# The second router's rows prepared in the last attention round, its logits by column tiles and a selection product

## The chip, the cores and the metric

The kernel runs on one core of a Trainium2 chip. The metric is device microseconds of one execution: 1426.83 us is the median of 3 runs of the kernel before (1425.14, 1426.83 and 1431.81).

## What is computed

A two-layer decoder over 2048 rows of 256 values (`x`) with 1601 context rows of 512. Each layer adds a cross-attention part and a mixture of eight experts; the change lies between the second layer's attention and its experts. Cut to that, the reference is:

```python
# attention of the second layer: 8 heads of 32, queries are the normed rows
x = x + jnp.tanh(g_xattn[1]) * attention(ctx_2048, _layernorm(x), mask)
...
def _L1_ffn_ref(x, rw1, rb1, rw2, rb2, w1, b1, w2, b2):      # x is layernorm(x)
    logits = jax.nn.silu(jnp.einsum('bsd,dh->bsh', x, rw1) + rb1)      # 256 -> 1024
    logits = jnp.einsum('bsh,he->bse', logits, rw2) + rb2              # 1024 -> 8
    k_logits, k_index = jax.lax.top_k(logits, 2)
    k_prob = jax.nn.softmax(k_logits, axis=-1)
    ...
    for e in range(E):
        we = jnp.sum(jnp.where(k_index_f == e, k_prob_f, 0.0), axis=-1)
        h = jax.nn.silu(xf @ w1[e] + b1[e]) @ w2[e] + b2[e]
        out = out + we[:, None] * h
x = x + jnp.tanh(g_ffn[1]) * _L1_ffn_ref(_layernorm(x), ...)
```

## The kernel before, in words

The program is written engine by engine; each engine (TensorE or PE, VectorE or DVE, ScalarE or ACT, GpSimd or POOL, and SyncE or SP, which issues most transfers) has its own list in a fixed order, and semaphores tie them together. All data is f32. The 2048 rows are 16 chunks of 128, kept in X; four chunks are a query group.

Stages in order: loads and the first attention part (a recurrence over the context, to about 106 us of the span), the first router and its table, 23 slots of the first expert stage (to about 417), the second attention, the second router, 39 slots of the second expert stage.

**The second attention** runs in 8 rounds (`interleaved`): round n takes a query group n // 2 and four of the eight heads. A round has 13 steps, one for each block kc of 128 keys. In a step PE makes four score products (`scores`, 128x512 each, ScalarE turns them into exponentials in a ring PT of 16 tiles, half of it in Z1 and half in WS0) and the values' products of the step before (`values`: four products of 32 columns at the positions 0, 32, 64, 96 of the array, written to four quarters of PSUM tile PB6), and every second step the column sums of the exponentials (`summed`, the same form with ones). For the other steps POOL adds exponentials up (ACC in WS0 and WS1) and one sum of those ends the round. Between the scores stands the search for maxima of the next round (`maxima`, PE and DVE); the last round has no next one, so its steps hold scores, values and sums alone. Behind a round ScalarE copies the result out (`attended`), PE turns it (`turned_out`), and DVE divides it and adds it into X (`into_x`, eight parts in the steps 2 and 3 of the next round, with the row statistics of the group's four chunks in every second round).

**The second router** starts when the last round and its `into_x` are through. DVE and POOL make 1/std of all 16 chunks (`inv_std`, `power`). Then for each of four groups: for each of four chunks DVE norms the rows (XR, line 908), PE turns them (`turned`, line 277), DVE copies them to XG (line 913), one chunk after the other; SP also stores each XR to xn1, from which the experts gather. PE then makes eight hidden products (line 547: 2 matmuls of 128x512, RW1 against XG), ScalarE applies SiLU (line 1060, two tiles HR), and after each PE makes a logits product (`lm`, line 526: the 8 columns of rw2s against HR, 8 partitions of PB6, accumulated over eight). DVE copies the 8x512 result (LT, line 918) and four transposes (line 555) put the logits of 128 rows on 128 partitions of PB7. After four groups the routing (`route`, from line 686) and PE's table products (line 357) give the experts' slots.

`turned` takes its PSUM tile from a ring of three and waits until the reader of its last content is done. The order of PE's router is that of its loops; SP's order is the list of its transfers, and a wait in it holds what stands behind.

**The second expert stage** fetches about 2.2 MB of weights and bias a slot. The first slot's weights are fetched when the attention ends; those of the second wait for the table, as the gathers of rows do. Results are added into `out` by scattered transfers.

## Time and profile before

| what | us or share |
|---|---|
| median of 3 runs | 1426.83 |
| the profiled execution, its own time | 1423.83 |
| its span, first to last instruction | 1422.0 |
| PE busy, matmuls / weight loads | 1213.8 / 861.3 |
| DVE, ACT, POOL busy | 519.3, 465.7, 479.2 |
| mean granted clock of PE | 0.926 of full speed |

The page gives busy times of the engines over the whole span; the windows give the same by stage, with the granted clock and the transfers' share. The chain of waits is followed back from the last instruction, each step to what released it. A timeline row gives start, duration, engine, line, operation, tile written and tiles read, the number of instructions in the row, and in brackets the idle time before it with what ended it. A f32 matmul is two records there (a transposing one is one), with the numbers of operand rows and columns. PEld is the weight load of PE.

### The profile page before, as it was taken

The numbers are of one execution on the slowest core, as the hardware profiler recorded it, in microseconds if no ns is written. First come the engines' busy times: TensorE is split into PE (matmuls) and PEld (weight loads), VectorE is DVE, ScalarE is ACT, GpSimd is POOL, SyncE is SP. The second block draws the span as 40 slices with busy tenths as digits, with TensorE's granted clock in tenths as the row PEclk, the third lists the DMA queues.
The fourth block names the chain that finished last, engine by engine and source line by source line (L and its number), as shares of the span: only waits on it lengthen the run. The fifth ranks groups of instructions, "written<-read, shape, count | busy, mean of one in ns | idle before, by whom it ended". The sixth has DMA issues, their size and how long they took to land.

```text
span 1422.0 us, 19271 instructions
## 1 busy us (share of the span) xinstructions
PE 1213.8 (85%) x7094; PEld 861.3 (61%) x7094; DVE 519.3 (37%) x1255; ACT 465.7 (33%) x1067; POOL 479.2 (34%) x495
## 2 busy tenths in 40 slices
PE   2365899999977899999999999968875999999985
PEld 2245899999964444454544544322225888888885
DVE  1574222221127876675675765011114010101000
ACT  2011122221101355655655556611110333323331
POOL 0150111111103366576666755700001223223231
PEclk9885799999996699999999999989885999999998
DMA  6114587888841000000000000020001899999994
GB/s 195 48 60 148 205 295 285 295 295 323 306 170 40 1 1 1 1 16 0 1 16 1 1 16 1 0 93 15 26 4 61 290 337 304 315 306 302 331 304 132
DMA packets 53978, 197.08 MB, mean 139 GB/s; under 512 B 8539, under 2 KB 34397, under 8 KB 38013
## 3 DMA queue, kind: packets, MB, share of 16 engines
q1 hardware_dynamic: 39584, 173.25, 34.4%
q0 software_dynamic: 10464, 18.36, 5.4%
q10 hardware_dynamic: 3836, 4.24, 0.9%
q8 instruction: 57, 0.93, 0.3%
q14 instruction: 37, 0.30, 0.1%
HBM read 179.44 MB, written 16.38 MB: 138 GB/s over the span
## 4 chain that ended last, share of the span: by engine, by line
PE 59%; DMA 20%; DVE 10%; issue 5%; ACT 3%; POOL 1%; SPq 1%; ACTq 0%; POOLq 0%; DVEq 0%
DMA out<-Z,SI 18%; PE PQ L392 13%; PE PB L497 7%; PE PQ L482 6%; PE PB L406 6%; PE PB L466 5%; PE PQ L547 5%; PE PB L277 4%; PE PB L487 4%; DVE Z L852 3%; PE PQ L466 2%; PE PB L526 2%; PE PB L357 1%; DVE SM L568 1%; POOL SM L1084 1%
## 5 line engine op out<-in xcount | busy, mean ns | idle before, releaser
L392 PE MATMUL PQ<-Z,WS 128*128 128x128 f32 x2720 | 328.5, 277 | 11.9 <-issue 10.7
L392 PEld LDWEIGHTS PQ<-Z,WS 128*128 128x128 f32 x2720 | 323.0, 193 | 25.0 <-issue 18.9
L406 PE MATMUL PB<-WS,Z 128*128 128x256 f32 x992 | 234.3, 379 | 0.0
L852 DVE TENSOR_REDUCE Z<-PB 128x1 f32<-128x402 f32 x340 | 183.4, 567 | 87.1 <-PE PB L466 85.9
L406 PEld LDWEIGHTS PB<-WS,Z 128*128 128x128 f32 x992 | 179.1, 190 | 19.3
L482 PE MATMUL PQ<-QS,KS 128*128 128x512 f32 x416 | 173.0, 437 | 7.3 <-ACT Z L1041 4.5
L979 ACT ACTIVATE Z<-PQ,WS 128x128 f32<-128x128 f32 x312 | 89.2, 368 | 204.4 <-PE PQ L392 204.4
L466 PE MATMUL PB<-KS,QS 128*128 128x402 f32 x340 | 132.9, 403 | 15.7 <-DVE Z L852 6.8
L482 PEld LDWEIGHTS PQ<-QS,KS 128*128 128x128 f32 x416 | 77.1, 190 | 104.8 <-issue 56.6
L1041 ACT ACTIVATE Z<-PQ 128x512 f32<-128x512 f32 x208 | 109.6, 603 | 85.1 <-PE PQ L482 84.9
L1041 ACT ACTIVATE WS<-PQ 128x512 f32<-128x512 f32 x208 | 109.2, 604 | 79.4 <-PE PQ L482 79.4
L1103 POOL DMA_INDIRECT Z<-xn,SI x62 | 60.9, 983 | 218.0 <-DVE SM L749 199.8
L1110 POOL DMA_INDIRECT out<-Z,SI x39 | 61.9, 1588 | 207.5 <-DMA out<-Z,SI 177.9
L792 DVE TENSOR_TENSOR Z<-PB,Z 128x256 f32<-128x256 f32 x39 | 16.6, 424 | 284.9 <-PE PB L406 284.9
L1173 POOL TENSOR_TENSOR WS<-WS,Z 128x512 f32<-128x512 f32 x80 | 100.5, 1286 | 41.4 <-ACT Z L1041 41.4
L1173 POOL TENSOR_TENSOR WS<-WS 128x512 f32<-128x512 f32 x80 | 100.5, 1287 | 39.5 <-ACT WS L1041 39.5
L852 DVE TENSOR_REDUCE Z<-PQ 128x1 f32<-128x402 f32 x172 | 97.5, 567 | 43.8 <-PE PQ L466 43.2
L781 DVE TENSOR_TENSOR Z<-Z,PQ 128x512 f32<-128x512 f32 x46 | 31.6, 687 | 179.0 <-PE PQ L392 179.0
L466 PEld LDWEIGHTS PB<-KS,QS 128*128 128x128 f32 x340 | 67.7, 199 | 47.2 <-DVE Z L852 33.4
L1110 POOL DMA_INDIRECT yd<-Z,SI x23 | 22.7, 987 | 216.0 <-DVE Z L789 216.0
L975 ACT ACTIVATE Z<-PQ 128x512 f32<-128x512 f32 x46 | 27.5, 597 | 151.7 <-PE PQ L392 151.7
L466 PE MATMUL PQ<-KS,QS 128*128 128x402 f32 x172 | 69.6, 404 | 7.6 <-DVE Z L852 4.0
(238 smaller groups left out, 1246.2 us busy)
## 6 DMA issues: line engine op xcount, KB each, us to landing
WS<-in_w SPq DMA_DIRECT2D x62, 1024.0 KB, 6.8
WS<-in_w SPq DMA_DIRECT2D x23, 2048.0 KB, 8.1
WS<-in_w SPq DMA_DIRECT2D x39, 1028.0 KB, 7.5
Z<-in_b SPq DMA_DIRECT2D x39, 128.0 KB, 6.7
X<-in_x SPq DMA_DIRECT2D x4, 512.0 KB, 10.5
xn<-WS SPq DMA_DIRECT2D x16, 128.0 KB, 1.7
WS<-yd SPq DMA_DIRECT2D x4, 512.0 KB, 5.9
out<-X SPq DMA_DIRECT2D x4, 512.0 KB, 2.9
```

Of the source, the lines that this page charges most:

```text
L392: t = e.matmul(bank[:, j * P:j * P + P], w[:, k, o:o + P], FXT[i % 2][:, k * P:k * P + P], start=k == 0, stop=k == 1)
L406: t = e.matmul(y, FS[c % 4][:, j * P:j * P + P], w[:, 4 * n + j, :], start=n == 0 and j == 0, stop=n == 1 and j == 3)
L466: e.matmul(PB[b][:, 0:PIECE], q[:, h, t4 * P:t4 * P + P], KS[:, 4 * hf + h, s * PIECE:(s + 1) * PIECE], start=True, stop=True).then_inc(t_ ...
L482: e.matmul(PB[g % 3], KS[:, 4 * (n % 2) + hh, kc * P:kc * P + P], QS[n % 2][:, hh, :], start=True, stop=True).then_inc(t_s, 1)
L497: e.matmul(PB[6][32 * hh:32 * hh + 32, :], V[:, kc, (4 * hf + hh) * 32:(4 * hf + hh) * 32 + 32], PT[(g + hh) % 16], start=kc == 0, stop=kc ...
L547: t = e.matmul(PB[m % 3], RW1[:, k, f * P:f * P + P], XG[g % 2][:, k, :], start=k == 0, stop=k == 1)
L852: e.tensor_reduce(MP[j % 2][:, i:i + 1], PB[bank_of["pc", r]][:, 0:PIECE], AX.X, ALU.max).then_inc(v_pc, 1)
L979: t = e.activation(FS[c % 4][:, j * P:j * P + P], PB[c % 4][:, j * P:j * P + P], ACT.Silu, bias=WS[i % 2][:, o:o + 1])
L1041: e.activation(PT[g % 16], PB[g % 3], ACT.Exp).then_inc(a_p, 1)
L1103: e.indirect_dma_start(FXL[i % 4], None, xn, bass.IndirectOffsetOnAxis(ap=tabi[:, i:i + 1].bitcast(U32), axis=0)).then_inc(d_xl[l][i % 4], 16)
L1110: e.indirect_dma_start(into, bass.IndirectOffsetOnAxis(ap=tabi[:, i:i + 1].bitcast(U32), axis=0), FY[i % 2], None, **add).then_inc(d_y[l][ ...
L1173: e.tensor_tensor(acc, acc, PT[g % 16], ALU.add).then_inc(p_acc, 1)
```

## The change

What it does:

- XR, XG and HR move: XR and XG lie in WS1, XG has four tiles in place of two (one for each group), HR has eight tiles in Z1 in place of two.
- In the last round, steps 1 to 12, `prepared` turns the chunks 0 to 11 behind each step's scores. DVE norms chunk c+1, then copies chunk c out. The 1/std of these chunks is made ahead of them, that of chunks 12 to 15 after the round; POOL's power is split in two.
- PE's router becomes one stream over 32 hidden products (`hidden`). The turning of the last attention output stands behind the second one. The chunks 12 to 15 are turned behind the 13th to 16th.
- The logits are made in eight groups of four products in column tiles (`partial_logits`): product j of a group writes partitions 32j to 32j+31, and the second half of a query group accumulates on the first. The weights RW2 are rw2 padded from 8 to 32 columns.
- DVE copies all 128 partitions (LT, `partial`), and `logits_of` makes for each chunk one product of LT with a constant 128x8 selection (C_SEL), which adds the four parts up and turns them at once, in place of the transpose.
- rw2 is no longer loaded at the start (1024 pieces of 32 B); RW2 is fetched to V when the last values are read. SP stores chunks 0 to 11 during the last round, 12 to 15 and the last part of X behind the first slot's weights.
- `route` waits for the stores of xn1 ahead of its first write to WS1.

PE, the start of the last round (line numbers differ by 2; lines 484 and 482 are scores, 499 and 497 values, 513 and 511 with the following row the turning of the output before). Before:

```order
L482 MATMUL PQ<-QS,KS 128x512 x4
L497 MATMUL PB<-WS,V 32x512 x4
L511 MATMUL PB<-CT,Z 128x128 x4
L277 MATMUL PB<-CT,Z 128x128 x4
L482 MATMUL PQ<-QS,KS 128x512 x4
L497 MATMUL PB<-Z,V 32x512 x4
```

Now:

```order
L484 MATMUL PQ<-QS,KS 128x512 x4
L279 MATMUL PB<-CT,WS 128x128 x2
L499 MATMUL PB<-WS,V 32x512 x4
L513 MATMUL PB<-CT,Z 128x128 x4
L279 MATMUL PB<-CT,Z 128x128 x4
L484 MATMUL PQ<-QS,KS 128x512 x4
L279 MATMUL PQ<-CT,WS 128x128 x2
L499 MATMUL PB<-Z,V 32x512 x4
```

Two transposes of a prepared chunk (from WS) have come in behind the scores of each of twelve steps.

PE, from the last column sums (487, now 489) into the router (547 and 526, now 538 hidden and 550 logits, 560 selection). Before:

```order
L487 MATMUL PB<-WS,CT 32x512 x8
L511 MATMUL PB<-CT,Z 128x128 x4
L277 MATMUL PB<-CT,Z 128x128 x4
L277 MATMUL PQ<-CT,Z 128x128 x2
L277 MATMUL PB<-CT,Z 128x128 x4
L277 MATMUL PQ<-CT,Z 128x128 x2
L547 MATMUL PQ<-Z 128x512 x4
L526 MATMUL PB<-Z,SM 8x512
L547 MATMUL PQ<-Z 128x512 x2
L526 MATMUL PB<-Z,SM 8x512
```

Now:

```order
L489 MATMUL PB<-WS,CT 32x512 x8
L538 MATMUL PQ<-WS,Z 128x512 x4
L513 MATMUL PB<-CT,Z 128x128 x4
L279 MATMUL PB<-CT,Z 128x128 x4
L538 MATMUL PQ<-WS,Z 128x512 x8
L550 MATMUL PB<-Z,V 32x512 x4
L538 MATMUL PQ<-WS,Z 128x512 x8
L550 MATMUL PB<-Z,V 32x512 x4
L538 MATMUL PQ<-WS,Z 128x512 x4
L560 MATMUL PB<-CT,Z 128x8 x4
```

The hidden products follow the sums at once, with the turning of the output behind the second, and the logits come in fours.

SP, around the end of the attention (out<-X are stored parts of X, xn<- the stored normed rows, in_w and in_b the weights and bias of a slot, in_rw the router's weights). Before:

```order
L1268 DMA out<-X 128x4x256 x4
L1221 DMA WS<-in_w 128x2056
L1226 DMA WS<-in_w 128x2048
L1230 DMA Z<-in_b 128x256
L1275 DMA xn<-Z 128x256 x16
```

Now:

```order
L1310 DMA out<-X 128x4x256 x3
L1316 DMA xn<-WS 128x256 x12
L1322 DMA V<-in_rw 128x8x32
L1263 DMA WS<-in_w 128x2056
L1268 DMA WS<-in_w 128x2048
L1272 DMA Z<-in_b 128x256
L1316 DMA xn<-WS 128x256 x4
L1310 DMA out<-X 128x4x256
```

Twelve stores of rows went ahead of the first slot's weights, RW2 came in, and one store of X went behind them.

The diff, its core:

```diff
@@ -57,6 +58,7 @@
...
+    c[:, C_SEL:C_SEL + E] = j[:, None] % 32 == np.arange(E)[None, :]
...
@@ -160,10 +162,11 @@
...
-        XR = [Z1[:, 256 * i:256 * i + 256] for i in range(4)]
-        XG = [Z1[:, 1024 + 1024 * i:2048 + 1024 * i].rearrange("p (k q) -> p k q", k=2) for i in range(2)]
-        HR = [Z1[:, 3072 + 512 * i:3584 + 512 * i] for i in range(2)]
-        LT = Z0[0:8, 2048:2560]
+        XR = [WS[1][:, 5120 + 256 * i:5376 + 256 * i] for i in range(4)]
+        XG = [WS[1][:, o:o + 1024].rearrange("p (k q) -> p k q", k=2) for o in (2048, 3072, 4096, 0)]
+        HR = [Z1[:, 512 * i:512 * i + 512] for i in range(8)]
+        RW2 = VW[:, 2560:2816].rearrange("p (f e) -> p f e", e=32)
+        LT = Z0[:, 2048:2560]
...
@@ -249,16 +252,15 @@
...
+                    if n == 7 and kc:
+                        prepared(kc - 1)
...
-                if kc == 1 and n:
+                if kc == 1 and n and n < 8:
...
-            turned_out(7)
-            for part in range(8):
-                into_x(7, part)
...
@@ -515,46 +517,61 @@
             for _ in maxima(0):
                 pass
...
+            def prepared(c):
+                e.wait_ge(v_xr, c + 1)
+                turned(ring, ("xr", c), [XR[c % 4][:, k * P:k * P + P] for k in range(2)],
+                       (v_xg, c + 1)).then_inc(t_xr, 1)
+            interleaved(maxima, scores, values, lambda n: None, turned_out, lambda n, part: None, prepared)
+            def hidden(m):
+                g, f = divmod(m, 8)
+                if f == 0:
+                    e.wait_ge(v_xg, 4 * g + 4)
+                if m == 0:
+                    e.wait_ge(d_rw1, 16)
+                    e.wait_ge(a_p, 416)
+                if m >= 3:
+                    e.wait_ge(a_hr, m - 2)
+                for k in range(2):
+                    t = e.matmul(PB[m % 3], RW1[:, k, f * P:f * P + P], XG[g][:, k, :], start=k == 0, stop=k == 1)
+                t.then_inc(t_hr, 1)
+            def partial_logits(h):
+                g, half = divmod(h, 2)
+                e.wait_ge(a_hr, 4 * h + 4)
+                if h == 0:
+                    e.wait_ge(d_rw2, 16)
+                    e.wait_ge(a_ot, 8)
+                if half == 0 and g:
                     e.wait_ge(v_lt, g)
...
+                for j in range(4):
+                    t = e.matmul(PB[6][32 * j:32 * j + 32, :], RW2[:, 4 * half + j, :], HR[(4 * h + j) % 8],
+                                 start=half == 0, stop=half == 1, tile_position=(0, 32 * j))
+                t.then_inc(t_lm, 1)
+            def logits_of(g):
+                e.wait_ge(v_lt, g + 1)
+                if g == 0:
+                    e.wait_ge(v_rt, 8)
                 for t4 in range(4):
                     c = 4 * g + t4
...
+                    t = e.matmul(PB[7][:, c * E:c * E + E], LT[:, t4 * P:t4 * P + P], CT[:, C_SEL:C_SEL + E], start=True,
+                                 stop=True)
                 t.then_inc(t_lt, 1)
...
+            for m in range(32 + 4):
+                if m < 32:
+                    hidden(m)
+                if m == 1:
+                    turned_out(7)
+                if m % 4 == 1 and m > 4:
+                    partial_logits((m - 5) // 4)
+                if m % 8 == 3 and m > 8:
+                    logits_of((m - 11) // 8)
+                if 12 <= m < 16:
+                    prepared(m)
             ranks(1)
             tables(1)
@@ -726,6 +743,9 @@
...
+                if l == 1:
+                    for i in range(4):
+                        e.wait_ge(d_xn[1][i], landed(NC - 1, 4))
...
@@ -893,29 +913,50 @@
             query_norms(0, 4)
             for _ in maxima(0):
                 pass
...
+            def normed(c):
+                if c == 0:
+                    e.wait_ge(p_pw, 7)
+                if c == 12:
+                    e.wait_ge(p_pw, 8)
+                if c >= 4:
+                    e.wait_ge(t_xr, c - 3)
+                    e.wait_ge(d_xn[1][c % 4], landed(c - 4, 4))
+                e.tensor_scalar(XR[c % 4], X[:, c, :], mean[:, c:c + 1], rst[:, c:c + 1], ALU.subtract,
+                                ALU.mult).then_inc(v_xr, 1)
+            def grouped(c):
+                e.wait_ge(t_xr, c + 1)
+                e.tensor_copy(XG[c // 4][:, :, c % 4 * P:c % 4 * P + P],
+                              PB[bank_of["xr", c]][:, 0:D].rearrange("p (k q) -> p k q", k=2)).then_inc(v_xg, 1)
+            def prepared(c):
+                if c == 0:
+                    inv_std(0, 12)
+                    normed(0)
+                if c < 11:
+                    normed(c + 1)
+                grouped(c)
+            interleaved(maxima, lambda *a: None, lambda *a: None, lambda n: None, lambda n: None, into_x, prepared)
+            for part in range(8):
+                into_x(7, part)
+            inv_std(12, NC)
             e.wait_ge(t_v, 640)
...
+            def partial(g):
+                e.wait_ge(t_lm, 2 * g + 2)
                 if g:
                     e.wait_ge(t_lt, g)
...
+                e.tensor_copy(LT, PB[6]).then_inc(v_lt, 1)
+            for c in range(12, NC):
+                normed(c)
+            partial(0)
+            for c in range(12, NC):
+                grouped(c)
+            for g in range(1, 4):
+                partial(g)
             e.wait_ge(t_lt, 4)
             route(1, rb2s, NT1, PB[7][:, 0:NC * E].rearrange("p (c e) -> p c e", e=E))
             experts(1, NT1, lambda c: None)
@@ -1049,15 +1090,15 @@
...
-            interleaved(maxima, scores, lambda *a: None, attended, lambda n: None, lambda n, part: None)
+            interleaved(maxima, scores, lambda *a: None, attended, lambda n: None, lambda n, part: None, lambda c: None)
...
-                if m >= 2:
-                    e.wait_ge(t_lm, m - 1)
-                e.activation(HR[m % 2], PB[m % 3], ACT.Silu, bias=rb1s[:, f:f + 1]).then_inc(a_hr, 1)
+                if m >= 8:
+                    e.wait_ge(t_lm, (m - 8) // 4 + 1)
+                e.activation(HR[m % 8], PB[m % 3], ACT.Silu, bias=rb1s[:, f:f + 1]).then_inc(a_hr, 1)
...
@@ -1159,6 +1200,8 @@
                         yield
             def scores(n, kc, hh):
+                if n == 7 and kc == 1 and hh == 0:
+                    power(rst[:, 0:12], 7)
                 if not on_pool(kc) or kc == 0:
                     return
                 g = 52 * n + 4 * kc + hh
@@ -1263,20 +1305,26 @@
...
-            for g in range(4):
+            def finished(g):
...
-            e.wait_ge(t_v, 640)
-            def stored():
-                for c in range(NC):
+            def stored(a, b):
+                for c in range(a, b):
...
+            for g in range(3):
+                finished(g)
+            stored(0, 12)
+            e.wait_ge(t_v, 640)
+            e.dma_start(RW2, rw2.rearrange("(f p) n -> p f n", p=P)).then_inc(d_rw2, 16)
...
-                    stored()
+                    stored(12, NC)
+                    finished(3)
...
@@ -1324,7 +1372,7 @@
...
-        "rw2": arr(L1_ffn_rw2, FF, E),
+        "rw2": np.pad(arr(L1_ffn_rw2, FF, E), ((0, 0), (0, 32 - E))),
...
```

## Rows read from the trace of the kernel before

**Rows 1.** The page, part 4: shares of the chain of waits.

```profile
PE 59%; DMA 20%; DVE 10%; issue 5%; ACT 3%; POOL 1%; SPq 1%; ACTq 0%; POOLq 0%; DVEq 0%
```

**Rows 2.** Windows: busy of the engines (x instructions), PE's granted clock, share of transfers, GB/s.

```profile
888.00:925.00 37.00, 33.85 (x203) 11.52 (x201) 1.99 (x3) 23.29 (x46) 28.61 (x23) 1.00 0.00 0
925.00:940.00 15.00, 3.91 (x17) 2.07 (x17) 7.04 (x20) 1.79 (x3) 2.93 (x1) 0.65 0.63 219
940.00:1056.50 116.50, 104.95 (x228) 31.59 (x228) 11.08 (x28) 23.20 (x33) 0.00 (x0) 0.90 0.04 14
...
1124.00:1420.00 296.00, 264.70 (x1767) 240.38 (x1765) 28.00 (x72) 91.04 (x318) 91.38 (x70) 0.98 0.92 293
```

**Rows 3.** Timeline, two steps of the last round; POOL's sums at 886 and 916.

```profile
886.21 5.44 POOL L1170 TENSOR_TENSOR WS<-WS,Z 128x512 f32<-128x512 f32 x4 [7.32 <-ACT Z L1041]
...
892.67 1.06 PE L497 MATMUL PB<-Z,V 128*32 128x512 f32 x8
...
893.55 1.04 PE L487 MATMUL PB<-Z,CT 128*32 128x512 f32 x8
...
894.52 0.96 PE L482 MATMUL PQ<-QS,KS 128*128 128x512 f32 x3
...
895.71 0.49 PE L482 MATMUL PQ<-QS,KS 128*128 128x512 f32 x1 [0.22 <-ACT WS L1041]
...
898.75 1.07 PE L497 MATMUL PB<-WS,V 128*32 128x512 f32 x8
...
916.59 4.99 POOL L1173 TENSOR_TENSOR WS<-WS 128x512 f32<-128x512 f32 x4 [1.08 <-ACT WS L1041]
```

**Rows 4.** The same timeline, output of the round before being turned, and what follows.

```profile
887.61 0.66 PE L511 MATMUL PB<-CT,Z 128*128 128x128 f32 x4
...
888.46 0.94 PE L482 MATMUL PQ<-QS,KS 128*128 128x512 f32 x3
```

**Rows 5.** Timeline, from the last column sums to the first turned chunks.

```profile
922.38 1.90 PE L487 MATMUL PB<-WS,CT 128*32 128x512 f32 x16
...
930.72 2.93 POOL L1084 TENSOR_TENSOR SM<-SM 128x16 f32<-128x16 f32 x1 [9.14 <-DVE SM L574]
...
935.68 0.69 PE L277 MATMUL PB<-CT,Z 128*128 128x128 f32 x2 [0.84 <-DVE Z L908]
```

**Rows 6.** Timeline, weight loads of the first group's second hidden product.

```profile
943.75 0.19 PEld L547 LDWEIGHTS PQ<-Z 128*128 128x128 f32 x1 [0.24 <-issue]
944.17 0.19 PEld L547 LDWEIGHTS PQ<-Z 128*128 128x128 f32 x1 [0.24 <-issue]
```

**Rows 7.** Chain in order of time (start, us, what), second and third group.

```profile
985.46 1.91 PE PQ L547 x4
987.37 0.95 PE PB L526 x2
...
993.11 1.83 PE PB L526 x4
...
1001.33 5.28 PE PQ L547 x8
```

**Rows 8.** Timeline, end of the router, routing and table.

```profile
1054.58 0.69 ACT L1060 ACTIVATE Z<-PQ,SM 128x512 f32<-128x512 f32 x1 [2.18 <-PE PQ L547]
...
1056.39 0.68 DVE L918 COPY Z<-PB 8x512 f32<-8x512 f32 x1 [24.41 <-PE PB L526]
...
1057.58 0.29 DVE L686 TENSOR_TENSOR SM<-PB,SM 128x128 f32<-128x128 f32 x1 [0.50 <-PE PB L555]
...
1077.67 13.94 PE L357 MATMUL PB<-V,WS 128*128 128x78 f32 x64 [12.36 <-DVE WS L738]
```

**Rows 9.** Chain in order of time, start of the program.

```profile
15.73 0.71 SPq L1199
...
16.49 7.78 DMA SM<-in_rb
```

**Rows 10.** Transfer queues, 22 to 24: packets, MB, share of 16 engines.

```profile
q1 hardware_dynamic: 989, 0.03, 28.2%
```

More of the change, by code:

```diff
@@ L33 @@
 C_PAD, C_LAST, C_UI, C_I128 = 1088, 1089, 1090, 1218
-C_N = 1346
-SMN = 3112
+C_SEL = 1346
+C_N = 1354
+SMN = 3048
 def constants():
@@ L181, in build @@
         d_yd = [sem(f"d_yd{g}") for g in range(4)]
-        d_rw1, d_res = sem("d_rw1"), sem("d_res")
+        d_rw1, d_rw2, d_res = sem("d_rw1"), sem("d_rw2"), sem("d_res")
         v_pad, p_set, a_tg = sem("v_pad"), sem("p_set"), sem("a_tg")
@@ L232, in on_pool, with interleaved @@
             return kc == 0 or kc % 2 == 1
-        def interleaved(maxima, scores, values, attended, turned_out, into_x):
+        def interleaved(maxima, scores, values, attended, turned_out, into_x, prepared):
             side = iter(())
@@ L517, in _ @@
                 pass
-            interleaved(maxima, scores, values, lambda n: None, turned_out, lambda n, part: None)
-            def lm(g, f):
-                m = 8 * g + f
-                e.wait_ge(a_hr, m + 1)
-                if f == 0 and g:
-                    e.wait_ge(v_lt, g)
-                e.matmul(PB[6][0:8, :], rw2s[:, 8 * f:8 * f + 8], HR[m % 2], start=f == 0, stop=f == 7).then_inc(t_lm, 1)
-            for g in range(4):
+            def prepared(c):
+                e.wait_ge(v_xr, c + 1)
+                turned(ring, ("xr", c), [XR[c % 4][:, k * P:k * P + P] for k in range(2)],
+                       (v_xg, c + 1)).then_inc(t_xr, 1)
@@ L529, in _ @@
+            def logits_of(g):
+                e.wait_ge(v_lt, g + 1)
+                if g == 0:
+                    e.wait_ge(v_rt, 8)
                 for t4 in range(4):
                     c = 4 * g + t4
-                    e.wait_ge(v_xr, c + 1)
-                    turned(ring, ("xr", c), [XR[c % 4][:, k * P:k * P + P] for k in range(2)],
-                           (v_xg, c + 1)).then_inc(t_xr, 1)
-                for f in range(9):
-                    if f < 8:
-                        m = 8 * g + f
-                        if f == 0:
-                            e.wait_ge(v_xg, 4 * g + 4)
-                        if m == 0:
-                            e.wait_ge(d_rw1, 16)
-                            e.wait_ge(a_p, 416)
-                            e.wait_ge(v_rt, 8)
-                            e.wait_ge(a_ot, 8)
-                        if m >= 3:
-                            e.wait_ge(a_hr, m - 2)
-                        for k in range(2):
-                            t = e.matmul(PB[m % 3], RW1[:, k, f * P:f * P + P], XG[g % 2][:, k, :], start=k == 0,
-                                         stop=k == 1)
-                        t.then_inc(t_hr, 1)
-                    if f >= 1:
-                        lm(g, f - 1)
@@ L552, in _ @@
-                e.wait_ge(v_lt, g + 1)
-                for t4 in range(4):
-                    c = 4 * g + t4
-                    t = e.transpose(PB[7][:, c * E:c * E + E], LT[:, t4 * P:t4 * P + P], ident[0:8, 0:8])
-                t.then_inc(t_lt, 1)
-            e.wait_ge(v_xg, NC)
+                    t = e.matmul(PB[7][:, c * E:c * E + E], LT[:, t4 * P:t4 * P + P], CT[:, C_SEL:C_SEL + E], start=True,
+                                 stop=True)
+                t.then_inc(t_lt, 1)
+            for m in range(32 + 4):
[9 more added lines that the diff above has]
+                    prepared(m)
@@ L628, in evac_dep @@
                 e.tensor_tensor(DR[c % 2], PB[6 + c % 2][:, 0:D], bIB, ALU.add).then_inc(v_dep, 1)
-            e.wait_ge(d_small, 192)
+            e.wait_ge(d_small, 176)
             for c in range(NK):
@@ L932, in _ @@
             e.dma_start(mski, kmask).then_inc(d_ctx, 16)
-            e.wait_ge(d_small, 192)
+            e.wait_ge(d_small, 176)
             e.wait_ge(p_set, 1)
@@ L1173, in scores @@
                     e.tensor_tensor(acc, acc, PT[g % 16], ALU.add).then_inc(p_acc, 1)
-            interleaved(maxima, scores, lambda *a: None, lambda n: None, lambda n: None, lambda n, part: None)
-            power(rst, 7)
+            interleaved(maxima, scores, lambda *a: None, lambda n: None, lambda n: None, lambda n, part: None, lambda c: None)
+            power(rst[:, 12:NC], 8)
             e.wait_ge(d_res, 64)
@@ L1263, in _ @@
             e.dma_start(RW1, rw1.rearrange("(k p) n -> p k n", p=P)).then_inc(d_rw1, 16)
-            for g in range(4):
+            def finished(g):
                 e.wait_ge(v_x3, 2 * g + 2)
```

21 lines of the change are left out of this document (1 added, 20 removed).

## The prediction

> **What bounds the kernel now.** I read the chain of waits first, then the windows by stage, then the timeline of the stages that the change touches. In the shares of the chain TensorE holds 59% and transfers 20% [rows 1]: for most of the span the end is set by what TensorE does or waits for. The windows say what each stage lacks [rows 2]. In the last attention round (888 to 925) PE is busy 33.85 of 37 us, DVE only 1.99: TensorE sets the pace, DVE has nothing to do. In 925 to 940 PE is busy 3.91 of 15 us: it waits. In 940 to 1056.5, the router's products, PE is busy 105 of 116.5 us, so that stretch costs what its matmuls cost. From 1124 on the transfers are busy 0.92 of the time at 293 GB/s: the second expert stage is bound by its weights.
>
> Nothing of that last stage is fetched ahead, but for the first slot's weights: the second slot waits for the table that follows the router, and so do the gathers. What the router gives back should therefore shift the rest of the program as a whole.
>
> **The stretch that is rewritten.** It reaches from the end of the last column sums, 922.38 + 1.90 = 924.28 [rows 5], to the first instruction of the routing, 1057.58 [rows 8]: 133.3 us before. Term by term, as the new order of TensorE has it:
> - Waits removed. After the last values PE waited for ScalarE's two copies, DVE's statistics, POOL's power of 2.93 us (from 930.72) [rows 5], then turned four chunks, each with a hand-over to DVE and back. Between two groups the same again: 993.11 + 1.83 to 1001.33, 6.4 us [rows 7]. Now the first 12 chunks are ready, and PE goes on with the hidden products. What is late next is chunks 12 to 15: before, DVE's and POOL's work on them had ended 9.4 us behind the last sums (930.72 + 2.93) [rows 5]; now it starts two hidden products later and ends some 13 us in, and is wanted only behind the 13th product, over 20 us in. Covered.
> - Hidden products: 32 of 2 f32 matmuls (4 records). Weight loads follow each other at 944.17 - 943.75 = 0.42 us [rows 6], so 4 records cost 1.71 if nothing is exposed; with a product of 8 columns in between they cost 1.91 [rows 7]. That is the pair of bounds. Mostly they now follow each other; I take 1.75, 56.0 us, and 0.2 us more for each of 8 returns from another tile shape, 1.6.
> - Logits: before 32 products of 8 columns at 0.95 us [rows 7], 30 us. Now 8 groups of four in column tiles. The same form stands in the last round: the values' group begins at 892.67, the sums' at 893.55, the next scores at 894.52, so the two groups cost 0.88 and 0.97 us [rows 3]. I take 1.0 each, 8.0 us.
> - Turning the attention's output, now behind the second hidden product: eight transposes in 888.46 - 887.61 = 0.85 us [rows 4].
> - Selection products: 4 matmuls (8 records) with a full weight load and 8 moving columns. No row has them. Nearest below is a transposing record at full clock, 0.85/8 = 0.106 [rows 4], 0.85 us for four; nearest above the table's record at the low clock, 13.95/64 = 0.218 [rows 8], 1.74 us. Three times inside the stream, near the lower: 2.6 us.
> - Turning chunks 12 to 15 inside the stream: 4 pairs at 0.3 (next part), 1.2 us.
> - The tail behind the last hidden product: SiLU 0.69 and its hand-overs, 0.9; DVE's copy 0.68 [rows 8] with hand-overs, 0.86; a last selection after a wait, between the bounds, 1.3. Together 3.1 us. That the copy has 128 partitions in place of 8 costs nothing by DVE's rows, where time goes with the columns.
>
> Sum 56.0 + 1.6 + 8.0 + 0.85 + 2.6 + 1.2 + 3.1 = 73.4 us, **59.9 us less**.
>
> Four products beside each other need not cost one. The rows put a visit with its group at 0.88 to 0.97 us, where a single product takes 0.85 to 0.95, and the sum above goes by them. The Trainium skill (TensorE: Matmul & The Clock Gate, Part 3, measured speedup) gives a factor of 3.07, not 4, for four tiles of this width of stream, and 2.38 for three column tiles. As an estimate by that page a group would take 4 x 0.85 / 3.07 = 1.11 us and the eight 0.9 us more than I take. The starts in rows 3 speak against it.
>
> **What the last round pays.** In 12 steps of that round PE gets two more transposes, behind the step's four scores. PE is the bound there, two steps take 898.75 - 892.67 = 6.08 us, and its only wait in a step, 0.22 us for ScalarE ahead of the fourth score [rows 3], lies before the transposes and can't hide them. In a stream two cost 2 x 0.106 = 0.21 us [rows 4]; alone, with the wait, 0.69 [rows 5]. I take 0.3, near the stream: 3.6 us (2.5 to 8.3; nought if the profile's idle time is more than it shows). The semaphore that they wait on is given one step ahead: DVE norms chunk c+1 before it copies chunk c, and it is idle. DVE's work on the attention output of the round before (its 1.99 us there [rows 2], in steps 2 and 3) stands between and fits in a step of 3 us. POOL's power must come before its first sum of this round; POOL was idle for 7.32 us ahead of that sum [rows 3], so the 2.9 us are hidden; if that cover were gone, up to 2.9 us. POOL's last sums end at 916.59 + 4.99 = 921.6, the products that need them start after 923.2 [rows 3, 5]: 1.6 us for whatever DVE's new work takes from POOL. On SP's queue three stores of X and twelve of 128 KB now stand ahead of the weights' loads; all are due before the round ends. The fourth store and the last four wait behind loads of 2 MB, and their takers (gathers, scatter-adds) come 70 us later.
>
> **The router's small weights** leave the start and are fetched, padded to 32 columns (1024 rows of 128 B), when the last values are read. PE wants them at the first group, 5 to 6 hidden products later (10 us): with a free queue, nothing. At the start they pay: ScalarE's first work waits for all small loads; SP issues this one in 0.71 us and the last, behind it, takes 7.78 us to land [rows 9]; its 1024 packets are among those that fill the queue to the end, 989 of them taking 28.2% of 2 us on 16 engines, 9 ns each [rows 10], so 0.6 us for 1024. What ScalarE does next hangs on the path to the first expert stage. Between 0 and 2.3 us (all of both and the uneven tail); I take 1.0. The constants grow by 8 columns of 1346: nothing.
>
> **Sum.** 59.9 - 3.6 + 1.0 = 57.3 us less. Against the profiled execution's own time, 1423.83: 1366.5. The median of the runs shown, 1426.83, lies 3.0 above that; in their terms 1369.5 us.
>
> Bounds. Downward: free turns in the round 3.6, hidden products at 1.71 with no returns 2.9, start 1.3, selections 0.4, and 1.7 for the spread below the median (its lowest run): to 1359. Upward: hidden products at 1.91 (5.1 less the 1.6 of returns), turns at 0.69 4.7, start 1.0, selections 2.6 and 0.4: to 1382.
>
> **Rivals.**
> - *The round waits for DVE.* If PE met each pair of turns before its chunk was normed, a step would cost the hand-over of before, 0.69 + 0.84 [rows 5] in place of 0.3: 12 times 1.23, 14.8 us, **1384**. Against it: DVE is idle and one step ahead. For it: the ring of four stored chunks, whose freeing goes through SP and a transfer. 5%.
> - *The column groups run one after the other.* Four times 0.85 in place of one: 8 x 2.55 = 20.4 us, **1390**. The sums of the same shape speak against it [rows 3]. 3%.
> - *The shift is not passed on.* If the expert stage lost half (its transfers at 0.92 [rows 2], other collisions with the scatter-adds): **1398**. Against it: all its loads start after the table, as before. 3%.
> - *Slower: TensorE at its lower clock.* In 925 to 940, after waits, the granted clock is 0.65, in the router 0.90, in the busy last round 1.00 [rows 2]; after each break the first 8 records take 5.28 us in place of some 3.5 [rows 7]. If the new stream ran at 1.2 GHz throughout, its PE time, 69.5 of the 73.4 us, would double: **1439**, slower than before. It decides from 57.3/69.5, 82% of the stream at the low clock. What fell was behind idle time, and the change takes that away. 2%.
>
> **How the numbers follow.** The forecast has 86%, the rivals 5, 3, 3 and 2, and 1% goes to a low clock for just so long that the gain is cancelled. Below and above the forecast's own bounds I leave little; the first rival ends at the upper edge, so 1359 to 1382 should hold it 8 times in 10. Within 0.5% (7 us) is what a measurement here can't tell from no change. The forecast and the first three rivals are faster by more: 0.97; slower 0.02; same 0.01.
>
> **What would show it.** The first hidden product right behind the last sums, the clock at 1.00 from 888 to the last hidden product, hidden products at 1.7 to 1.9 us, groups of four at about 1.0; the last round some 3 us longer, the routing's first instruction some 57 us earlier, and the stage behind it as long as before. I would be wrong if PE waits for DVE in the round's turns, for the small weights in the first group, or if the expert stage has grown.

## The result, and the profile after

The changed kernel takes **1367.57 us** (median of 4 runs, 1365.88 to 1368.55), the kernel before 1425.99 beside it (4 runs): a ratio of 0.9597, 95% interval 0.9574 to 0.9620, 58.4 us less. Forecast were 1369.5 us, in 1359 to 1382. The profiled execution took 1368.55 us, its span is 1366.8 and its mean granted clock 0.932 (before: 1423.83, 1422.0 and 0.926).

Page of the changed kernel, part 4, shares of the chain of waits (before: [rows 1]):

```profile
PE 66%; DMA 14%; DVE 10%; issue 4%; ACT 3%; POOL 1%; SPq 1%; ACTq 0%; POOLq 0%; DVEq 0%
```

These shares tell little by themselves: another execution of the same code (run 1 below) had 59 and 20%. In the last stage transfers and TensorE are close, and now the one, now the other ends last. The stages say more. Windows of the changed kernel (start:end, length, busy time of PE, PEld, DVE, ACT and POOL with their instructions, granted clock, share of transfers, GB/s):

```profile
888.00:926.00 38.00, 35.57 (x224) 13.95 (x222) 10.84 (x24) 22.73 (x44) 28.69 (x23) 1.00 0.11 35
926.00:940.00 14.00, 14.00 (x47) 6.14 (x44) 5.34 (x16) 6.49 (x9) 1.02 (x1) 1.00 0.65 221
940.00:998.00 58.00, 56.41 (x198) 24.05 (x196) 4.46 (x8) 19.14 (x27) 0.00 (x0) 1.00 0.02 6
1064.00:1366.00 302.00, 267.72 (x1777) 244.26 (x1776) 28.45 (x74) 90.95 (x318) 91.28 (x70) 0.98 0.89 289
```

Against [rows 2]: in the last round DVE is busy 10.84 us where it had 1.99, which is the norming and copying out of the chunks. Behind the round TensorE is busy all of 14 us, where it had 3.91 of 15, and its clock stays at 1.00 up to the last hidden product. The last stage looks as it did.

**The last round.** Timeline of the changed kernel, the same two steps as in [rows 3] (line 484 scores, 279 the new turns, 499 values, 489 sums; 924 and 929 are DVE's norm and copy; 1125 POOL's power):

```profile
877.84 0.95 PE L484 MATMUL PQ<-QS,KS 128*128 128x512 f32 x3
...
878.55 2.30 POOL L1125 TENSOR_TENSOR SM<-SM 128x12 f32<-128x12 f32 x1
...
885.91 5.44 POOL L1213 TENSOR_TENSOR WS<-WS,Z 128x512 f32<-128x512 f32 x4 [5.05 <-ACT Z L1082]
...
892.38 0.50 PE L484 MATMUL PQ<-QS,KS 128*128 128x512 f32 x1 [0.22 <-ACT WS L1082]
892.72 0.38 PE L279 MATMUL PB<-CT,WS 128*128 128x128 f32 x2
893.02 1.07 PE L499 MATMUL PB<-Z,V 128*32 128x512 f32 x8
893.13 0.42 DVE L929 COPY WS<-PB 128x256 f32<-128x256 f32 x1 [0.98 <-PE PB L279]
893.47 0.41 DVE L924 TENSOR_SCALAR WS<-X,SM 128x256 f32<-128x256 f32 x1
...
899.54 1.06 PE L499 MATMUL PB<-WS,V 128*32 128x512 f32 x8
```

The scores that stand at 877.84 here, in the kernel before:

```profile
878.14 0.95 PE L482 MATMUL PQ<-QS,KS 128*128 128x512 f32 x3
```

No wait for DVE stands ahead of the turns: the chunk that is turned at 892.72 was normed by 891.50. Two steps take 899.54 - 893.02 = 6.52 us in place of 6.08, so a pair of turns costs 0.22. The last of the twelve pairs costs hardly anything. From these scores to the end of the last sums it is 926.39 - 877.84 = 48.55 us, and before it was 924.28 - 878.14 = 46.14: the round pays 2.4 us. POOL's power of 2.30 us runs while POOL would be idle, and 5.05 us of idle time are left behind it.

**The router.** Chain in order of time of the changed kernel (start, us, what; 538 hidden products, 513 and the first 279 the turning of the attention's output, 550 the logits in column tiles, 560 the selection, 1101 SiLU, 951 DVE's copy, 703 the routing's first instruction):

```profile
924.67 1.72 PE PB L489 x16
926.39 3.63 PE PQ L538 x8
930.02 0.44 PE PB L513 x4
930.46 0.44 PE PB L279 x4
930.89 6.87 PE PQ L538 x16
937.76 1.00 PE PB L550 x8
938.76 7.06 PE PQ L538 x16
...
950.45 0.79 PE PB L560 x8
951.24 1.82 PE PQ L538 x4
953.06 0.22 PE PQ L279 x2
953.28 1.72 PE PQ L538 x4
...
994.30 0.70 ACT Z L1101
...
995.04 1.11 PE PB L550 x8
...
996.18 0.70 DVE Z L951
...
996.92 1.29 PE PB L560 x8
...
998.24 0.30 DVE SM L703
```

The first hidden product starts where the last sums end, at 926.39. Each takes 1.72 us (6.87 for four) and 0.1 to 0.2 more behind logits or selection products. That is no price of the column tiles: in run 2 below, which has none, four behind logits products take the same 7.06. A group of four logits products costs 1.00 us. From 926.39 to 998.24 it is 71.9 us, where it was 133.3.

The routing begins at 998.24 in place of 1057.58, 59.3 us earlier, yet this span is only 55.2 us shorter: from there to the end it is 368.6 us here and 364.4 before. In the other runs of this study that leave this stage as the change has it (the first four and the eighth below) it took 364.2, 360.9, 363.0, 365.2 and 370.4, a mean of 365.4 with this one; in two profiles of the kernel before 364.4 and 366.7. The stage scatters by some 10 us and did not grow.

### The profile page after: what moved, and what is told of

It is laid out like the page before. It is cut to its first block, busy times and chain, and to the rows that moved or that the text cites. A ratio compares the mean times of both kernels' runs of the same rounds, so it can differ in the third digit from the quotient of the medians.

```text
span 1366.8 us, 19293 instructions
## 1 busy us (share of the span) xinstructions
PE 1180.5 (86%) x7110; PEld 863.4 (63%) x7110; DVE 520.4 (38%) x1256; ACT 465.5 (34%) x1067; POOL 479.6 (35%) x496
## 4 chain that ended last, share of the span: by engine, by line
PE 66%; DMA 14%; DVE 10%; issue 4%; ACT 3%; POOL 1%; SPq 1%; ACTq 0%; POOLq 0%; DVEq 0%
PE PQ L394 16%; DMA out<-Z,SI 10%; PE PB L408 10%; PE PB L499 7%; PE PQ L484 7%; PE PB L468 5%; PE PQ L538 4%; PE PB L279 4%; PE PB L489 4%; DVE Z L872 3%; PE PQ L468 2%; DMA Z<-xn,SI 2%; PE PB L359 2%; DVE SM L585 1%; PE PQ L279 1%
## 5 line engine op out<-in xcount | busy, mean ns | idle before, releaser
L408 PE MATMUL PB<-WS,Z 128*128 128x256 f32 x992 | 237.1, 383 | 0.0
```

What stands on the lines that cost most here:

```text
L408: t = e.matmul(y, FS[c % 4][:, j * P:j * P + P], w[:, 4 * n + j, :], start=n == 0 and j == 0, stop=n == 1 and j == 3)
```

## The experiments

| run | executions | us, median (range) | ratio to before, 95% |
|---|---|---|---|
| r1_as_changed | 4 | 1365.62 (1363.96 to 1368.25) | 0.9574 (0.9539 to 0.9609) |
| r2_untiled | 4 | 1381.67 (1378.94 to 1391.14) | 0.9706 (0.9658 to 0.9753) |
| r3_unprepared | 4 | 1372.55 (1370.63 to 1379.63) | 0.9630 (0.9585 to 0.9675) |
| r4_both_undone | 4 | 1390.39 (1388.27 to 1392.64) | 0.9740 (0.9705 to 0.9774) |
| r5_warm | 6 | 1361.20 (1354.99 to 1363.77) | 0.9534 (0.9504 to 0.9563) |
| r6_fetch | 5 | 1363.27 (1361.18 to 1365.18) | 0.9552 (0.9523 to 0.9580) |
| r7_warm_fetch | 5 | 1364.02 (1361.21 to 1364.38) | 0.9552 (0.9523 to 0.9580) |
| r8_small_load | 1 | 1371.27 | |
| r9_warm14 | 4 | 1356.39 (1351.63 to 1360.03) | 0.9519 (0.9477 to 0.9560) |
| r10_before_again | 1 | 1425.74 | |
| r11_warm_two | 5 | 1355.71 (1352.39 to 1359.89) | 0.9531 (0.9508 to 0.9554) |
| r12_warm14_fetch | 5 | 1359.47 (1354.09 to 1360.58) | 0.9537 (0.9512 to 0.9563) |

The kernel before took 1427.45 us beside the first four, 1426.76 beside the fifth to the eighth, 1427.08 beside the ninth and tenth, 1424.08 beside the last two.

**The changed kernel once more**, as the base of what follows.

> The changed kernel once more, for its spread and for the length of its last stage. Theory (the whole gain reaches the end; the last stage's length varies from run to run with its transfers): within 3 us of 1367.6, and the stretch from the routing's first instruction to the end somewhere between 364 and 369 us, where the profile of before had 364.4 and that of the changed kernel 368.6. Rival (the change itself made the last stage 4 us longer): 368 to 369 us again.

1365.62 us, 61.8 less than before. From the routing's first instruction to the end it is 364.2 us, so the 368.6 of the first profile were scatter.

**Column tiles undone.** The four products write the same 8 partitions one after the other, and a transpose takes the place of the selection:

```diff
-                    t = e.matmul(PB[6][32 * j:32 * j + 32, :], RW2[:, 4 * half + j, :], HR[(4 * h + j) % 8],
-                                 start=half == 0, stop=half == 1, tile_position=(0, 32 * j))
+                    t = e.matmul(PB[6][0:8, :], RW2[:, 4 * half + j, 0:8], HR[(4 * h + j) % 8],
+                                 start=half == 0 and j == 0, stop=half == 1 and j == 3)
```

> The groups of four stay where they are, but as four products of 8 columns one after the other, turned by transposes. Theory (four column tiles cost one streaming of 512 columns): each group grows from 1.00 to about 3.5 us, 8 x 2.5 = 20 us slower than the changed kernel, about 1387. Rival (a good part of the old cost per logits product was the exposed weight load at each change of shape, and is gone by the grouping alone): under 15 us slower.

Chain in order of time of this run; the lines are those of the chain above:

```profile
930.68 6.87 PE PQ L538 x16
937.55 3.53 PE PB L550 x8
941.08 7.06 PE PQ L538 x16
```

A group of four products costs 3.53 us one after the other (with 8 columns of weights each) and 1.00 beside each other (with 32). Between last sums and routing there are 18.3 us more, and the median rises by 16.0. The eight groups alone would give 8 x 2.53 = 20.2; the transposes give some 2 back, since four of them take 0.34 us in the stream where four selections take 0.79, and less in the tail. The rival of the sequential tiles is out: a group would have cost what it costs here. So the four tiles run at once but for 1.00 - 3.53/4, about 0.12 us: a factor of 3.5. The Trainium skill (TensorE: Matmul & The Clock Gate, Part 3, measured speedup) gives 3.07 for four row tiles and 2.38 for three column tiles. The prediction set the 1.11 us a group that it estimated by the 3.07 beside its own 1.0 from [rows 3], and the trace bears out the rows.

**The preparing in the round undone.** The chunks 0 to 11 are normed and turned behind the round; the tiles and the order of the stream stay.

```diff
-            interleaved(maxima, scores, values, lambda n: None, turned_out, lambda n, part: None, prepared)
+            interleaved(maxima, scores, values, lambda n: None, turned_out, lambda n, part: None, lambda c: None)
+            for c in range(12):
+                prepared(c)
```

(DVE the same: `inv_std(0, 12)` stays in the round, `normed` and `grouped` come behind it.)

> Chunks 0 to 11 are turned behind the last round in place of inside it, normed one ahead; column tiles stay. Theory (in the round they cost 0.22 us each on PE, outside the chain of DVE and PE with PE's clock falling behind it): the last round 2.3 us shorter, then 12 chunks at 0.9 to 1.5 us, 11 to 18 us, and 2 us for hidden products at the low clock: 11 to 18 us slower, 1379 to 1386. Rival (PE pays for the turns wherever they stand): under 5 us slower.

Timeline of this run, from the last sums on (926 and 931 are DVE's norm and copy):

```profile
921.74 1.90 PE L489 MATMUL PB<-WS,CT 128*32 128x512 f32 x16
923.78 0.73 DVE L926 TENSOR_SCALAR WS<-X,SM 128x256 f32<-128x256 f32 x2 [33.92 <-PE PB L489]
...
927.69 0.40 DVE L926 TENSOR_SCALAR WS<-X,SM 128x256 f32<-128x256 f32 x1
928.01 0.41 DVE L931 COPY WS<-PB 128x256 f32<-128x256 f32 x1
928.14 0.44 PE L279 MATMUL PB<-CT,WS 128*128 128x128 f32 x2 [0.22 <-DVE WS L926]
...
932.73 0.41 DVE L926 TENSOR_SCALAR WS<-X,SM 128x256 f32<-128x256 f32 x1 [1.25 <-DMA xn<-WS]
...
933.67 6.23 PE L540 MATMUL PQ<-WS,Z 128*128 128x512 f32 x8
```

Two windows of this run (columns as above):

```profile
926.00:930.00 4.00, 2.95 (x12) 1.38 (x12) 3.87 (x13) 0.17 (x1) 0.00 (x0) 0.84 0.60 198
930.00:934.00 4.00, 2.29 (x8) 1.39 (x8) 2.17 (x7) 0.00 (x0) 0.00 (x0) 0.50 0.31 103
```

The theory holds in kind and misses in size: 6.9 us by the medians, where 11 to 18 were expected, and more than the rival's 5. The twelve chunks take 923.78 to 933.9, 10.1 us. With four tiles XR and a ring of PSUM tiles the norm of one chunk runs beside the turn of the one before, and a chunk costs what DVE's two instructions, which overlap a little, take: 0.65 us from one norm to the next. I had priced it by the full hand-over there and back of [rows 5]. The last chunk also waits 1.25 us for the store that frees its XR. The clock falls while it lasts: it is 1.00 from 923.6 to 926, where TensorE is busy half of the time, and 0.50 from 930 to 934. The first two hidden products take 6.0 us for 3.6. Last sums to routing is 12.9 us longer; the round gives 2.4 back, since it no longer holds the turns. That makes 10.5. In the profiles the stage behind takes 363.0 us here, 364.2 and 368.6 in the changed kernel; the rest of the difference to 6.9 is put down to that scatter and not shown otherwise.

**Both undone.**

> Both of the above. Theory (the parts lie on one chain and add up): the sum of the two, 31 to 38 us slower, 1399 to 1406, so that some 20 us of the gain stay: the waits between groups, the output's turn under the hidden products, and the clock. Rival (they overlap, since a longer stream of PE hides the turns): less than the sum by 5 us or more.

24.8 us over the changed kernel, where 16.0 + 6.9, some 23, are the two alone: within the noise they add. The 31 to 38 us expected were too much mostly because the turns had been priced too high, as in run 3. And 37.1 us of the gain by the medians (32.1 by the profiles, last sums to routing) need neither tiles nor preparing. They belong to the single stream: to hidden products and logits that no longer take turns one by one, to the three waits of 6.4 us between groups [rows 7] and the slow records behind each of them, and to the attention's output, which is copied, turned and added while hidden products run. The three waits alone are 3 x 6.4 = 19 us; how the rest divides was not tried.

**Warming products.** Behind the routing's start nothing was changed, and there TensorE stood idle before the table at the low clock. Products whose result nobody reads fill the time:

```diff
+            def warm(k):
+                for _ in range(k):
+                    e.matmul(PB[3], CT[:, C_U:C_U + P], CT[:, 0:512], start=True, stop=True)
+            warm(5)
             ranks(1)
+            warm(12)
             tables(1)
+            warm(3)
```

> The changed kernel with 20 products of constants into an unused PSUM tile while PE waits: 5 behind the last selection, 12 behind the rank products, 3 behind the table. Theory (what is left between router and experts is paid at the low clock, as the first groups were before): the 64 table records fall from 13.95 us to 7.5 at full clock, the first slot's 16 records from 3.8 to 1.8, so 6 to 9 us faster than the changed kernel, 1357 to 1361. Rival (the products of constants end late and hold up the rank or table products, or the last stage is set by its transfers and gives nothing on for the first slot): 0 to 4 us.

The time fell by 4.4 us by the medians, but the main term of what was expected did not come. The first gather of rows starts only 0.9 us earlier (1032.50 for 1033.40). The first slot is the faster one: its first 16 records take 2.05 us for 3.78, and the third slot's weights are issued 2.8 us earlier (1042.13 for 1044.94). First the table in the profile of the changed kernel, then the same line in this run, then two windows of this run (columns as above):

```profile
1018.28 13.94 PE L359 MATMUL PB<-V,WS 128*128 128x78 f32 x64 [12.36 <-DVE WS L758]
```

```profile
1017.92 13.39 PE L359 MATMUL PB<-V,WS 128*128 128x78 f32 x64 [2.09 <-DVE WS L765]
```

```profile
1018.00:1020.00 2.00, 2.00 (x12) 2.00 (x13) 2.00 (x2) 0.00 (x0) 0.00 (x0) 0.64 0.00 0
1020.00:1024.00 4.00, 4.00 (x20) 4.00 (x20) 2.13 (x5) 0.00 (x0) 0.00 (x0) 0.50 0.00 0
```

The clock was at 1.00 behind the twelve products and through the 2.09 us of idle time, and fell to 0.50 (1.2 GHz) within the table; it stayed there although the 64 records left no gap. Run 7, with the same twelve products, shows the same: 2.09 us idle, 13.34 us for the table. Either that idle time dropped the clock, or the records would do so by themselves; run 9 tells the two apart.

**The second slot's weights before the table.** Lanes and hot of the second table move from WS1 to Z1 and Z0, so that the second slot's weights can come to WS1 while the routing runs:

```diff
-            lanes = WS[1][:, 4096 - cc * P:4096].rearrange("p (q n) -> p q n", n=P)
-            hot = WS[1][:, 4096:4096 + cc * nt].rearrange("p (q t) -> p q t", t=nt)
+                lanes, hot = Z1[:, 0:cc * P], Z0[:, 0:cc * nt]
...
-                    e.wait_ge(t_tab[1], 1)
-                    e.wait_ge(d_xl[1][0], 16)
+                    e.wait_ge(t_hr, 32)
+                    for k in range(4):
+                        e.wait_ge(d_xn[1][k], landed(NC - 1, 4))
```

> The routing's scratch moves out of WS1 (to Z1 and Z0), so that the second slot's weights are fetched when the last hidden product is done, some 38 us earlier, in place of behind the table. Theory (the last stage is bound by its 2.2 MB a slot at some 300 GB/s): one slot's transfer fewer in it, 6 to 7.5 us faster than the changed kernel. Rival (the first slots are bound by PE at 7.2 us each and the scatter-adds set the rest): 0 to 2 us, and the profile's last stage as long as before.

Issues of weights in the changed kernel (the first part of the second slot's and of the third's), then in this run:

```profile
1036.37 0.33 SPq L1263 DMA_DIRECT2D WS<-in_w  x1
...
1044.94 0.33 SPq L1263 DMA_DIRECT2D WS<-in_w  x1
```

```profile
994.20 0.33 SPq L1267 DMA_DIRECT2D WS<-in_w  x1
...
1044.86 0.33 SPq L1267 DMA_DIRECT2D WS<-in_w  x1
```

The load is issued 42 us earlier, but the third slot's comes when it did, so nothing behind it moves. The time is 2 us lower, with intervals that overlap: the rival's 0 to 2.

**Both of these.**

> Both of the above. Theory (the warm table shifts the whole stage, the fetch shortens it): the gains add, 12 to 16 us faster than the changed kernel, about 1352. Rival: no more than the better of the two alone.

1364.02 us, 0.8 and 2.8 above the two alone: nothing is gained on top of either, as the rival had it. The third slot's weights are issued at 1042.34, in run 5 at 1042.13.

**The small weights back at the start**, loaded there in 32-byte pieces beside what the change does:

```diff
+            e.dma_start(rw2s.rearrange("p (k n) -> p k n", k=8), rw2[:, 0:E].rearrange("(k p) n -> p k n", p=P)).then_inc(d_small, 16)
```

> The changed kernel with the 1024 pieces of 32 B of rw2 loaded at the start again (unused). Theory (they stand ahead of the last small load that ScalarE's first work waits for): ScalarE's tanh goes from 25.9 back to 26.4 us, 0.5 us, and no more. Rival (the shift came from other causes, such as the order in which the queues are served): it stays within 0.2 us of 25.9.

The last small load lands at 24.20 in place of 23.73 us and ScalarE's tanh starts at 26.38 for 25.91. Two runs without that load started as late (26.18 in run 3, 26.44 in run 6), so that the load causes the half microsecond is not shown, and it is at most that. The one execution's time, 1371.27 us, can't settle so small a difference.

**Fourteen warming products in place of twelve**, which closes the idle time ahead of the table:

```diff
-            warm(12)
+            warm(14)
```

> As the run with warming products (5, 12 and 3 products of 128x512 whose result nobody reads, around the ranks and the table products), but 14 in place of 12 ahead of the table. There TensorE stood idle for 2.09 us between the last of the 12 and the first table record, and its clock fell to 0.64 and 0.50 within the table products, whose 64 records took 13.39 us. If that idle time is what drops the clock: 14 products end 1.7 us later, 0.3 us ahead of the table's operands, the granted clock stays at 1.00 through the table and the 64 records take 6.9 to 8 us, so that the table is ready 5 to 6 us earlier and the kernel takes 1356 to 1360 us (against 1361.2 with 12). Rival: the table products keep the array too lightly busy themselves, whatever stands ahead of them: their 64 records take 13 us again and the time stays at 1359 to 1364 us.

Timeline of this run:

```profile
1017.37 7.37 PE L359 MATMUL PB<-V,WS 128*128 128x78 f32 x64 [0.36 <-DVE WS L765]
...
1025.93 1.11 POOL L1151 DMA_INDIRECT Z<-xn,SI  x1 [89.89 <-DVE SM L776]
...
1035.08 0.33 SPq L1270 DMA_DIRECT2D WS<-in_w  x1
```

The theory held: with 0.36 us of idle time ahead of them the same 64 records take 7.37 us at a granted clock of 1.00, in place of 13.39. Runs 11 and 12, with the same fourteen products, show 0.36 and 7.37 again. So the records alone don't drop the clock. The first gather of rows starts at 1025.93, in the changed kernel at 1033.40, 7.5 us later; the third slot's weights are issued at 1035.08 for 1044.94, 9.9 us earlier. The kernel takes 1356.39 us, 9.2 less than run 1 by the medians and 7.8 by the ratios (0.9574 and 0.9519), whose intervals overlap a little. The interval of this run overlaps that of run 5 as well. That fourteen products beat twelve at the end of the kernel, and not only in the table, rests on all runs that have them: the eleven executions with twelve (runs 5 and 7) took 1361.5 us on average, the fourteen with fourteen (9, 11 and 12) 1356.8.

**The kernel before, again**, for its last stage.

> The kernel before, unchanged, for its last stage: from the routing's first instruction to the end of the span it took 364.4 us, and the changed kernel 368.6 us in its profile, but 356 to 370 us in the profiles of its variants. If that stage merely scatters, this one lies anywhere from 356 to 370 us; if the change had made it longer, it would lie at 364 us again, below every profile of the variants that left the stage as the change has it.

366.7 us: inside the scatter of 356 to 370, and above 364. The 356 is that of run 5, which changed the stage's start; the variants that did not have 360.9 to 370.4, and 366.7 lies in that too.

**Warming in the first router too**: 4 products ahead of its ranks and 9 ahead of its table.

> As the run with 14 warming products, and the same in the first router, where TensorE waits 3.63 us ahead of the ranks and 8.08 us ahead of the table, whose 32 records took 7.06 us at the low clock: 4 and 9 products more. If idle time is what drops the clock there too: the 32 records take 3.5 to 4 us, the kernel 3 to 5 us less than with the second router's alone, 1352 to 1354 us. Rival: the stage behind is fetched by then only in part, or the products come out longer than the waits: 1355 to 1359 us.

Timeline of this run (350 and 351 are the ranks' products, 365 the warming ones):

```profile
130.35 6.18 PE L365 MATMUL PQ<-CT 128*128 128x512 f32 x8
136.36 0.39 PE L350 MATMUL PB<-SM,CT 128*128 128x128 f32 x2
...
145.06 3.77 PE L359 MATMUL PB<-WS 128*128 128x46 f32 x32 [0.36 <-DVE WS L767]
...
153.74 6.47 PE L400 MATMUL PQ<-Z,WS 128*128 128x128 f32 x32 [0.47 <-ACT Z L1017]
...
160.04 0.38 PE L279 MATMUL PB<-CT,Z 128*128 128x128 f32 x2
```

The table took 3.77 us in place of 7.06. But the four products ahead of the ranks ran at the low clock, 6.18 us for a wait of 3.63, and the ranks came 2.8 us late. 1.1 us of gain was left at the first slot's first products (153.74 for 154.88 in the changed kernel), and they lost it again: the 32 records took 6.47 us for 5.28, and what follows them starts at 160.04 for 159.99. Here no products stood behind the table. The time can't be told from run 9. At that clock, 1.5 us a product, two would have fitted.

**Fourteen products and the early fetch.**

> As the run with 14 warming products, and the second slot's weights fetched before the table. With the table 6.6 us earlier, the stage begins sooner and its transfers bound it; the early fetch gave 2 us alone and nothing on top of 12 products. If the first slots wait for weights: 1353 to 1356 us. Rival: what bounds the stage is the sum of its transfers after the table, of which this takes one slot in 39 away, hidden in the scatter: 1355 to 1358 us.

1359.47 us, above both ranges, and a ratio of 0.9537: the fetch adds nothing. The lowest medians are those of runs 9 and 11, 1356 us, some 9 us below the changed kernel; by their ratios they can't be told from runs 5 and 12.

## Why the prediction was right

By its own terms, against the profile (the hidden products are what is left of 926.39 to 994.30 without the output's turning, seven groups, three selections and four turns):

| term | forecast, us | measured |
|---|---|---|
| hidden products and returns | 57.6 | 56.7 |
| logits in column tiles | 1.0 each | 1.00 (one after the other 3.53) |
| turning the output | 0.85 | 0.87 |
| three selections in the stream | 2.6 | 2.4 |
| turns of chunks 12 to 15 | 1.2 | 1.0 |
| tail | 3.1 | 2.9 |
| last sums to routing | 73.4 | 71.9 |
| turns in the last round | +3.6 | +2.4 |
| start | -1.0 | at most -0.5 |
| routing starts earlier by | 57.3 | 59.3 |

- **The waits removed** were the surest term and held: no gap at 926.39, and chunks 12 to 15 are turned without a wait behind the 13th to 16th product. Run 3 shows what stands there otherwise.
- **The column groups** were read from the rows of the values and sums, which have the same shape. Run 2 measured the other way: the 20.4 us that the rival charged are 20.2 for the groups themselves.
- **Hidden products** took the lower bound, 1.72 us, and the returns 0.1 to 0.2: the 1.75 that I took as a middle was 0.9 us too much in all.
- **The round** cost less than I took, 0.22 for 0.3 a pair: the transposes cost in the stream what they cost in any stream, and the 0.22 us for ScalarE stood ahead of them as before.
- **The start** gave at most half of what I took. The last round's first scores come 0.3 us earlier than before in the profile (877.84 for 878.14), and 0.8 later in that of run 1 (878.96), so this term can't be told from scatter. With 0.3 the errors add up to the 2 us in 59: 1.5 too much for the stretch, 1.2 too much for the round, 0.7 too much gain at the start.
- **Luck** has a share in how near the time came. By the profiles the span is 55.2 us shorter and not 59.3, since the last stage came out 4 us longer in that one; by the medians it is 58.4. With a last stage that scatters by some 10 us, a forecast right to 2 us is better than its terms can promise; the terms themselves, each read from its own rows, are not luck.
- **The rest of the program shifted whole.** The rival in which the expert stage gives back half is out: in the profiles it took on average what it took before. That this stage is bound by its weights, as the prediction reads [rows 2], is not borne out: TensorE is busy 0.89 of it too, and run 6 took one slot's transfer out of its start and moved nothing behind it. The sum did not rest on it.
- **The low clock**: the stream ran at 1.00 throughout. Where run 3 puts waits back, the clock falls, to 0.50 within some 6 us of the last sums. That rival had its mechanism right, and the condition for it was taken away by the change.

## What to carry to other kernels

Products that wait on another engine one by one are worth gathering into one stream, with each hand-over placed some products ahead of its use: that alone was more than half of the gain here, before any tiling. Where the stationary operand has few columns, four of them side by side in column tiles cost hardly more than one. And where TensorE must wait and its next work decides the end, fill the wait nearly whole (with 0.36 us left the clock held here, with 2.09 it did not), and only with as many products as fit at the clock that they will run at.

## What the runs showed of the hardware

- The clock's fall is decided by little: twelve products and 2.09 us of idle time gave a table of 13.39 and 13.34 us (runs 5 and 7), most of it at 1.2 GHz, fourteen and 0.36 us one of 7.37 three times (runs 9, 11 and 12). At 1.2 GHz 64 records without a gap didn't bring it back.
- Idle time alone doesn't decide it. In runs 11 and 12 TensorE waited 1.26 us ahead of the rank products and the clock stayed at 1.00. There the five products before them had run at 1.00; where the same five ran in runs 5, 7 and 9, from 998 to 1004, the mean was 0.72 or 0.73 and no wait was left. What makes that difference between runs of the same instructions was not found.
- DVE's norm in the round took 0.40 to 0.49 us, but once 1.36, beside one of POOL's four sums that took 5.44 together, 1.36 each. It is the same norm (at 890.14 in the changed kernel) in all ten profiles that keep the preparing in the round (there 1.36 or 1.37 us). The Trainium skill (GPSIMD Engine Reference, Specifications) says that GpSimd shares its interfaces to SBUF with VectorE, with contention for DVE instructions in a 2-port perf mode or with two SBUF inputs; this row may be such a case, while other norms beside POOL's sums, of the same form, were not held up. What sets it was not tried.
- The last stage of the same code took 360.9 to 370.4 us from one profile to the next. Of a single profiled execution, a difference of 4 us behind the routing says nothing.
